# Second normalisation in two halves, with the first set of projections between them

## What is computed

```
def _gn(v):                      # over all tokens, for each channel
    return (v - mean) / sqrt(var + 1e-5)

x = x + attention(_gn(x))        # layer 0: LayerNorm, q k v, bias, softmax, gate, out
x = x + triangle(_gn(x))         # layer 1

# triangle:
zn  = layernorm(z, ln_in_w, ln_in_b)              # over 32 channels of a token
a   = mask * sigmoid(zn @ a_g_w + a_g_b) * (zn @ a_p_w + a_p_b)
b   = mask * sigmoid(zn @ b_g_w + b_g_b) * (zn @ b_p_w + b_p_b)
x   = einsum('bikh,bjkh->bijh', a, b)
xn  = layernorm(x, ln_out_w, ln_out_b)
out = sigmoid(zn @ g_w + g_b) * (xn @ z_w + z_b)
```

## Time and profile before

| | us |
|---|---|
| median of 3 runs | 285.29 (284.13 to 285.58) |
| the profiled execution, its own time | 284.4 |
| its span, first to last instruction | 282.6 |
| attention loop ends | about 205 |
| first matmul of L1060 | 210.6 |
| last channel sum (L805) | 218.7 to 219.4 |
| multiplications (L812) | 220.8 to 224.4 |
| transposes (L1081) | 221.5 to 226.5 |
| first set of projections, end | 229.3 |
| triangle matmuls start | 248.8 |
| last output stores issued | 278.4 |

### The profile page before, as it was taken

The page is one execution under the profiler, slowest core; times in us unless marked ns, Lnnn a source line. Parts: engine busy times, 40 slices in busy tenths (PEclk is TensorE's granted clock), DMA queues, the critical chain, the costliest instruction groups (busy, mean ns, idle before and its releaser), DMA issues.

```text
span 282.6 us, 6859 instructions
## 1 busy us (share of the span) xinstructions
PE 226.4 (80%) x2394; PEld 182.6 (65%) x2394; DVE 210.6 (75%) x368; ACT 209.2 (74%) x953; POOL 144.4 (51%) x132
## 2 busy tenths in 40 slices
PE   0589492469999999999999999999669599677930
PEld 0579230347888878888788887888459566376930
DVE  4047962357999999999999999998545739959790
ACT  0566643279999999999999999999545645569590
POOL 5400000008876777767777677766200019998081
PEclk9999668579999999999999999999958689965695
DMA  8400033534454643554445553330000000000038
GB/s 130 63 11 2 1 112 121 171 124 142 145 171 170 221 163 132 199 181 165 165 149 195 184 186 118 117 115 2 0 2 0 0 2 2 1 1 2 0 49 118
DMA packets 42389, 27.09 MB, mean 96 GB/s; under 512 B 24404, under 2 KB 42356, under 8 KB 42356
## 3 DMA queue, kind: packets, MB, share of 16 engines
q1 hardware_dynamic: 36572, 25.95, 28.8%
q10 hardware_dynamic: 5784, 0.71, 1.7%
HBM read 1.36 MB, written 1.18 MB: 9 GB/s over the span
## 4 chain that ended last, share of the span: by engine, by line
PE 31%; issue 27%; ACT 21%; DVE 12%; POOL 4%; SPq 3%; POOLq 1%; DMA 0%; DVEq 0%; ACTq 0%
ACT maps L659 17%; PE psum L1181 7%; PE psum L1060 3%; PE psum L1192 3%; PE psum L1145 2%; SPq L392 2%; DVE u_full L951 2%; PE psum L1248 2%; PE psum L1171 2%; DVE shared L991 2%; PE psum L1226 2%; PE psum L1231 2%; PE psum L1146 1%; PE psum L1148 1%; PE psum L1257 1%
## 5 line engine op out<-in xcount | busy, mean ns | idle before, releaser
L659 ACT ACTIVATE maps<-psum,neg_max 96x96 f32<-96x96 f32 x384 | 123.9, 353 | 4.9 <-DVE neg_max L928 4.1
L490 POOL TENSOR_TENSOR maps<-maps,rden 96x768 f32<-96x768 f32 x48 | 70.5, 1469 | 81.5 <-DVE rden L938 75.3
L659 ACT ACTIVATION_READ_ACCUMULATOR maps<-psum,neg_max 96x1 f32 x384 | 83.9, 219 | 0.0
L944 DVE COPY turned<-psum 96x1024 f32<-96x1024 f32 x48 | 58.5, 1219 | 8.4 <-PE psum L1181 8.4
L928 DVE TENSOR_REDUCE neg_max<-psum 96x8 f32<-96x768 f32 x48 | 45.7, 953 | 5.1 <-PE psum L1148 4.9
L1145 PE MATMUL psum<-u_st,x_stack 128*96 128x384 f32 x96 | 37.8, 394 | 10.4 <-DVE bias_lo L913 8.1
L1181 PE MATMUL psum<-ident,maps 96*96 96x96 f32 x384 | 40.0, 247 | 0.3 <-POOL maps L490 0.3
L1146 PE MATMUL psum<-bias_hi,ident_r 128*96 128x384 f32 x96 | 33.7, 351 | 0.0
L1148 PE MATMUL psum<-bias_lo,ident_r 128*96 128x384 f32 x96 | 33.4, 348 | 0.0
L1181 PEld LDWEIGHTS psum<-ident,maps 96*96 96x96 f32 x384 | 32.0, 126 | 0.5 <-POOL maps L490 0.5
L1145 PEld LDWEIGHTS psum<-u_st,x_stack 128*96 128x96 f32 x96 | 15.9, 166 | 19.8 <-issue 10.5
(11 more groups left out here) (178 smaller groups left out, 424.1 us busy)
## 6 DMA issues: line engine op xcount, KB each, us to landing
u_st<-u_split SPq DMA_DIRECT2D x96, 192.0 KB
x_stack<-shared SPq DMA_DIRECT2D x40, 96.0 KB, 2.0
maps<-in_x SPq DMA_DIRECT2D x4, 288.0 KB, 5.1
x_stack<-shared SPq DMA_DIRECT2D x4, 144.0 KB, 2.1
out_y<-maps SPq DMA_DIRECT2D x6, 96.0 KB, 3.1
out_y<-maps ACTq DMA_DIRECT2D x6, 96.0 KB, 3.4
bias_lo<-gate_sb SPq DMA_DIRECT2D x24, 12.0 KB
x_stack<-shared SPq DMA_DIRECT2D x4, 48.0 KB, 1.9
```

Of the source, the lines that this page charges most:

```text
L490: pool.tensor_tensor(at, at, rden[:, rows, :].unsqueeze(3).to_broadcast([N, 2, H, N]), ALU.mult).then_inc(probs_ready, 1)
L659: e = act.activation(probs[:, k % SLOTS, n, h], bank_s[r % 4][0:N, h * N:(h + 1) * N], ACT.Exp, bias=neg_max[:, r % BODY, h:h + 1], accum_ ...
L944: dve.tensor_copy(turned[0:N, j % 2].rearrange("p r x -> p (r x)"), psum[0:N, 2 * BANK:4 * BANK]).then_inc(t_ready, 1)
```

## The change

Layer 1 now handles its quads in two parts, 0 to 2 and 3 to 5; layer 0 keeps one part.

- DVE: three sums, the inverse root on 48 columns, three multiplications, and then the same again for the other three quads.
- ACT: the first root stands between the squares of quads 3 and 4; behind the two copies for the output weights stand the `zn_copy` of quads 0 to 2, then the second root, the load of the sigmoid's table and the other three `zn_copy`. Two roots instead of one: the counts that later waits use move by one.
- PE: transposes of quads 0 to 2, projections of set 0, transposes of quads 3 to 5, projections of set 1, then the other six sets. Set 0 waits for the copies of quads 0 to 2 only.
- Banks: so that set 0 can write banks 0 to 3 while quads 3 to 5 still stand in PSUM, these go to banks 4 to 6 (`d_bank`), and the transposes of the six quads go to banks 3, 7, 3, 7, 4, 7 (`turn_bank`). The wait for `res_copied` stands before quad 3 instead of quads 4 and 5.

The core of the diff:

```
+        def parts(layer):
+            return (range(QUADS // 2), range(QUADS // 2, QUADS)) if layer else (range(QUADS),)
+        def d_bank(q, layer):
+            return q + 1 if layer and q >= QUADS // 2 else q
+        TURN_BANKS = (3, 7, 3, 7, 4, 7)
+        def turn_bank(q, layer):
+            return TURN_BANKS[q] if layer else 6 + q % 2
...
 (ACT)
                 for q in range(QUADS):
+                    if layer and q == QUADS // 2 + 1:
+                        token_root(parts(1)[0], 4)
                     act.wait_ge(d_done, QUADS * layer + q + 1)
...
                     act.activation(z_const, bank_w[0:N, HD:2 * HD], ACT.Copy).then_inc(z_prep_copied, 1)
-                act.wait_ge(var_ready, 2 * layer + 2)
-                act.activation(tok[:, 2], tok[:, 1], ACT.Sqrt).then_inc(root_ready, 1)
+                    for q in parts(1)[0]:
+                        zn_copy(q)
+                token_root(parts(layer)[-1], 3 * layer + 2)
+
+            def token_root(quads, count):
+                at = slice(4 * quads[0], 4 * quads[-1] + 4)
+                act.wait_ge(var_ready, count)
+                act.activation(tok[:, 2, at], tok[:, 1, at], ACT.Sqrt).then_inc(root_ready, 1)
...
-            for q in range(QUADS):
+            for q in parts(1)[1]:
                 zn_copy(q)
...
 (DVE)
+                for part, quads in enumerate(parts(layer)):
+                    for q in quads:
+                        at = slice(4 * q, 4 * q + 4)
+                        dve.wait_ge(d_squared, QUADS * layer + q + 1)
+                        ins = dve.tensor_reduce(...)
+                    link(ins)
+                    inverse_root(quads, 2 * layer + 2 + part)
+                    for q in quads:
...
 (PE)
-                    if layer and q in (res_bank(n) for n in range(RES_EARLY, QUADS)):
+                    if layer and q == QUADS // 2:
                         pe.wait_ge(res_copied, QUADS)
...
-                need(pe, read, q - 1)
-                if layer and q == 1:
-                    pe.wait_ge(z_prep_copied, 1)
+                if layer:
+                    last = [n for n in range(q) if turn_bank(n, 1) == turn_bank(q, 1)]
+                    need(pe, read, last[-1] + 1 if last else 0)
+                    if q == 1:
+                        pe.wait_ge(z_prep_copied, 1)
+                else:
+                    need(pe, read, q - 1)
...
-            for q in range(QUADS):
-                block_transposes(q, 1, zn_ready)
-            for n in range(SETS):
-                if n < 2:
-                    pe.wait_ge(normed, 2 * QUADS)
-                    pe.wait_ge(zn_ready, QUADS if n else 1)
+            for n, quads in enumerate(parts(1)):
+                for q in quads:
+                    block_transposes(q, 1, zn_ready)
+                pe.wait_ge(normed, QUADS + quads[-1] + 1)
+                pe.wait_ge(zn_ready, quads[-1] + 1)
+                project(n)
+            for n in range(2, SETS):
                 project(n)
```

More of the change, by code:

```diff
@@ L583, in norm_front @@
                 for q in range(QUADS):
+                    if layer and q == QUADS // 2 + 1:
+                        token_root(parts(1)[0], 4)
                     act.wait_ge(d_done, QUADS * layer + q + 1)
                     act.activation(work[:, 4 * q:4 * q + 4].rearrange("j b f c -> j (b f c)"),
-                                   banks[q][0:N, :], ACT.Square).then_inc(d_squared, 1)
+                                   banks[d_bank(q, layer)][0:N, :], ACT.Square).then_inc(d_squared, 1)
                     if not layer and q < GROUP:
@@ L592, in norm_front, with zn_copy @@
                     act.activation(z_const, bank_w[0:N, HD:2 * HD], ACT.Copy).then_inc(z_prep_copied, 1)
-                act.wait_ge(var_ready, 2 * layer + 2)
-                act.activation(tok[:, 2], tok[:, 1], ACT.Sqrt).then_inc(root_ready, 1)
+                    for q in parts(1)[0]:
[5 more added lines that the diff above has]
+                act.activation(tok[:, 2, at], tok[:, 1, at], ACT.Sqrt).then_inc(root_ready, 1)
+            def zn_copy(q):
+                act.wait_ge(transposed, QUADS + q + 1)
+                act.activation(zn_t[:, 4 * q:4 * q + 4, :].rearrange("p b j -> p (b j)"), banks[turn_bank(q, 1)][:, 0:GN],
+                               ACT.Identity, scale=w_all[:, PW:PW + 1], bias=w_all[:, PW + 1:PW + 2]).then_inc(zn_ready, 1)
             def first_weights():
@@ L717, in _ @@
                                ACT.Copy).then_inc(tn_ready, 1)
-            act.wait_ge(var_ready, 5)
+            act.wait_ge(var_ready, 6)
             act.activation(tok[:, 2], tok[:, 1], ACT.Sqrt).then_inc(root_ready, 1)
@@ L801, in norm_front @@
                     z_preparation()
-                for q in range(QUADS):
[L803 to L814, removed]
-                                          ALU.mult).then_inc(normed, 1)
-                    else:
-                        dve.tensor_tensor(by_blocks(square)[:, at],
-                                          banks[q][0:N, :].rearrange("j (b c f) -> j b c f", c=C, f=GROUP),
-                                          tok[:, 3, at].unsqueeze(2).to_broadcast([N, 4, C, GROUP]),
-                                          ALU.mult).then_inc(normed, 1)
@@ L828, in z_preparation, with inverse_root @@
+            def inverse_root(quads, count):
+                at = slice(4 * quads[0], 4 * quads[-1] + 4)
+                dve.tensor_scalar(tok[:, 1, at], tok[:, 0, at], 1.0 / C, EPS, ALU.mult, ALU.add).then_inc(var_ready, 1)
+                dve.wait_ge(root_ready, count)
+                link(dve.reciprocal(tok[:, 3, at], tok[:, 2, at]))
             def z_preparation():
```

24 lines of the change are left out of this document (16 added, 8 removed).

## The result

| | before | after |
|---|---|---|
| median | 284.96 us (284.13 to 285.58, 4 runs) | 281.3 us (280.81 to 282.41, 4 runs) |
| ratio | | 0.988, 95% interval 0.984 to 0.992 |
| profiled execution, own time | 284.4 | 280.81 |
| its span | 282.6 | 279.0 |
| mean granted clock | 0.886 | 0.878 |

The mean clock over the span doesn't show what the change does: it also counts a low stretch ahead of the edited part, which ran from 200.93 to 214.58 in this execution and from 204.43 to 214.67 in the one before. "Weights' end" is the end of PE's matmuls for the output weights (L1070, now L1095), the last work ahead of the transposes.

What follows compares the result with a forecast made beforehand. The prediction took the serial chain of second normalisation, transposes and first projections, up to the mask of set 1, as the bound. 3.3 us earlier less 0.2 given back gave 285.29 - 3.1 = 282.2 us, range 281.0 to 284.5.

Steps and rivals of the forecast that it cites:

- sum: Whole kernel: 3.3 us gained at the mask of set 1, less 0.2 given back in the pipeline, makes 3.1.
- slack ahead of the second root: On ACT: first three zn copies end at 221.1, second root is wanted at 221.8, so 0.7 us of slack.
- the cover: On ACT: table load and dummy end at 223.5, before the fourth quad is transposed at 223.75; otherwise up to 1.5 us.
- Its split: Of 3.3 us at the mask of set 1, about 1.0 is the new order, 2.3 the full clock.
- first rival: PE's clock falls between the bursts of transposes and projections: gain 2.2, 0.8 or 0.2 us by how long; chance 0.24.
- a set costs 2.78 at the low clock: On PE: one set's projections take 2.78 us at the low clock, against about 2.2 at the full clock.
- low until set 1, gain 1.0 at the mask of set 1: Clock low through transposes and set 0: mask of set 1 at 230.3, 0.8 us left in all, 284.5.
- the rival's case with one slow set: Clock falls at 221.5, back by 225, first projection 2.78: gain 2.4 at the mask of set 1, 283.1 in all.
- the rival in which all sets stay slow: Clock stays low in the projections, six sets cost 3.5 us: 3.3 slower, 288.6; chance 0.05.
- POOL and DVE hold each other up: In the pipeline: long DVE products cost 2.0 us, 284.0; waiting whole POOL instructions, 0.8 slower, 286.1; chance 0.08.
- The slower case: Clock stays low in the projections after the mask of set 1: 3.3 us slower, 288.6; chance 0.05.
- It does nothing: Mask of set 1 stays at 231.34 through 1.9 us of new wait, such as a held-up second root; chance 0.01.

Runs made afterwards that it cites:

- fourth experiment: The changed kernel, unedited, timed and profiled again, against the kernel before: 282.03 us over 12 runs, ratio 0.9918.
- second experiment: The changed kernel with set 0 put behind all six quads of transposes, against the kernel before: 284.54 us, ratio 0.9994.
- sixth: The changed kernel with extra matmuls in PE's two gaps and POOL's constants of sets 5 to 7 later, against the kernel before: 281.47 us, ratio 0.9907.
- eighth: Changed kernel plus gap-filling matmuls, later POOL constants, quads transposed into their own banks, quad 4 copied by DVE; against the kernel before: 281.05 us, ratio 0.9894.

## Why the prediction was right, and where it was not

By its own steps, each read from the same point before and after, so that the unedited part ahead cancels:

| step | predicted | measured |
|---|---|---|
| first half's inverse, behind the start of the third sum | 1.63 | 1.66 |
| last product ends, behind the same | 8.43 | 8.25 |
| set 0 starts, behind the weights' end | 2.54 | 2.56 |
| last transposes end, behind the same | 6.44 | 6.50 |
| set 1 starts, behind the same | 7.24 | 7.36 |
| mask of set 1, behind the same | 9.49 | 9.51 |
| gain there | 3.3 | 3.27 |
| mask of set 1 to the triangle matmuls | 17.5 to 17.7 | 17.67 |
| sum | 3.1 | 3.27 - 0.23 = 3.04 |

**DVE** was bounded from 96 columns and from one, and the values between the bounds were met: 0.18, 0.24 and 0.45 against 0.18, 0.24 and 0.46. That the root path is paid twice costs nothing at the end, since the last product ends no later against the third sum than said. The 0.18 us that it came earlier lie mostly between like instructions, which overlap a little: three sums take 1.86 and not 3 x 0.68, three products 1.88.

**ACT** had less slack ahead of the second root than said, but enough. The copies of the first half end at 220.10, the second root starts at 220.64: 0.54 instead of 0.7. The table load and its dummy end at 222.39, and the fourth quad's copy starts at 222.85, so the cover holds by 0.46, more than the 0.25 that was worked out.

**The clock** was the step with the largest part, and its sign and size hold where the clock holds. Its split was 1.0 for the order and 2.3 for the clock. In the old order the clock alone brings 1.97, and 12.70 - 10.55 = 2.15 with the halves; with the clock held, the new order brings 1.3 (0.26 for the halves and 1.04 for the place of set 0). These lie near the split, but they are not what it says, and the likeness is in part luck. The prediction took the new order at the low clock for its 1.0. The fourth experiment is nearest to that and kept 0.48, so that in the new order the clock is worth 2.79. What the order is worth depends on the clock, and the split rests on a price that was too low, as follows.

**Two terms of the first rival were mis-sized.** Its chance was 0.24, and 2 of the 4 profiles of the changed kernel show it, too few to name a rate. And its price was too low: "a set costs 2.78 at the low clock" came from set 0 in the earlier trace rows, but the clock rose at 228.33, 0.24 us after L1231 started, so that row's 1.18 is nearly all full clock; and its 1.60 counts from the end of the transposes, while the four matmuls take 1.90. The second experiment shows a set wholly at the low clock, 1.90 + 1.93 = 3.8 us. So "low until set 1, gain 1.0 at the mask of set 1" should have been nearer to none, and the fourth experiment, in which the clock even came back between the sets, kept 0.48. The run with only set 1 slow kept 12.78 - 11.08 = 1.70, where the rival's case with one slow set said 2.4. The forecast of 3.3 itself used no such price, and so it stood; the rival in which all sets stay slow used it too, and would have cost more than said.

**The rest of the difference is not the change.** The spans differ by 3.62 us and the change accounts for 3.04. The quads' matmuls started 1.62 earlier, in a part that is not edited; 0.75 of it was given back at once, since the clock rose at about 214.6 in both profiles, so that more of these matmuls ran at the low clock; and the stretch from the triangle matmuls to the first store is 0.29 longer. 1.62 - 0.75 + 3.27 - 0.23 - 0.29 = 3.62. The two comparisons of the changed kernel say 3.4 (4 runs) and 2.3 (12 runs). The predicted 3.1 lies between them and within both intervals, but neither falls into the 2.9 to 3.5 that had a chance of 0.62. So the steps of the sum were right for an execution that keeps the clock; that the first comparison came out so near is in part luck, since the sum had no term for the executions that lose it.

**The other rivals.** POOL and DVE hold each other up about as much as before: four long products of eight, and 0.23 us given back. The slower case did not come: in the two profiles where the clock fell it was back (at 230.25 and 231.26) 0.2 us ahead of the end of set 1 and 0.9 behind it. "It does nothing" comes near in the fourth experiment, though not by the wait that was named, but by the clock.

The text predicted a clock of 1.00 from 216 to 245: it fell at 245.30. One thing behind the pipeline was not "as it was": PE idled 4.47 us ahead of the triangle matmuls, not 3.7: its last set ended at 240.39, and DVE's last product at 244.71.

## What to carry over

When a gap on TensorE closes, ask what the clock does with and without it, and price work at the low clock only from a row that ran at it from start to end; a row in which the clock rises gives too little. Before reordering for it, fill the gap with unused matmuls: that one run shows what the clock alone is worth in the old order, here 1.8 us where the change brought 2.3. Profile a kernel whose gain hangs on the clock several times, before and after: one profile here said 9.5 and another 12.3. And read a moved stretch from a fixed point near it, since the start of the stretch alone moves by over 2 us between executions.

## What the hardware showed that was not expected

- One program, unchanged, has outcomes that differ by 2.8 us in a stretch of 10 (9.51 to 12.30), by whether TensorE's granted clock holds through and behind two gaps of 0.85 us between groups of matmuls. The gap ahead of each set is 0.85 us where it held and where it fell. What tells these executions apart stays open.
- At the low clock the twelve small matmuls of a set (24 records) take 1.93 us against 1.07, the four long ones 1.90 against 1.09.
- Two instructions that start 0.03 us apart on DVE and POOL cost 1.08 us on DVE or 0.52 on POOL, by who is first, and only the first of these was on the path to the end. In both profiles with a shortened stage ahead of them and no wait (the sixth and eighth experiments) that order was turned round, and 1.1 of the 1.4 us were given back; one wait set it right.
